# A fused decoder layer on one core: first transposition of the probabilities behind the first scores, and VectorE's first key remainders behind the reciprocals

## The reference, cut to what matters

```python
sim = jnp.einsum('bhid,bhjd->bhij', q, k) * SCALE
attn = jax.nn.softmax(sim, axis=-1)
out = jnp.einsum('bhij,bhjd->bhid', attn, v)
x = _layernorm(x + out_projected)
```

## Time and profile before

| | us |
|---|---|
| median of 3 runs | 1244.94 (1244.93 to 1247.97) |
| the profiled execution, its own time | 1244.77 |
| its span (first to last instruction) | 1242.9 |
| TensorE busy | 1201.6 (97%) |
| VectorE busy | 863.6 (69%) |
| ScalarE busy | 555.1 (45%) |
| GpSimd busy | 584.7 (47%) |

### The profile page before, as it was taken

The page is one execution under the profiler, slowest core; times in us unless marked ns, Lnnn a source line. Parts: engine busy times, 40 slices in busy tenths (PEclk is TensorE's granted clock), DMA queues, the critical chain, the costliest instruction groups (busy, mean ns, idle before and its releaser), DMA issues.

```text
span 1242.9 us, 27255 instructions
## 1 busy us (share of the span) xinstructions
PE 1201.6 (97%) x10512; PEld 1050.0 (84%) x10512; DVE 863.6 (69%) x1694; ACT 555.1 (45%) x1097; POOL 584.7 (47%) x968
## 2 busy tenths in 40 slices
PE   8986999999999999999999999989999999999998
PEld 7865888888888888888888888877799899899888
DVE  5555988989889889889888898988523423432435
ACT  2123556555555555565565555545523412421420
POOL 2233665666666566656666576655322112202201
PEclk9997999999999999999999999999999999999999
DMA  9821012011111111120110111310222011021001
GB/s 274 225 63 35 20 51 61 19 60 44 35 52 53 34 54 44 35 60 20 60 50 30 59 46 35 125 39 26 95 69 69 1 69 69 1 69 69 1 1 35
DMA packets 88740, 70.07 MB, mean 56 GB/s; under 512 B 41379, under 2 KB 82084, under 8 KB 88613
## 3 DMA queue, kind: packets, MB, share of 16 engines
q1 hardware_dynamic: 86580, 67.67, 17.9%
q10 hardware_dynamic: 2032, 0.66, 0.2%
HBM read 42.09 MB, written 26.22 MB: 55 GB/s over the span
## 4 chain that ended last, share of the span: by engine, by line
PE 70%; POOL 8%; issue 8%; DVE 6%; ACT 1%; POOLq 0%; DVEq 0%
PE sim L137 6%; PE sim L138 6%; PE sim L139 6%; PE ob L137 5%; PE ob L139 5%; PE ob L138 5%; PE pt L499 4%; PE pw L393 3%; PE pt L139 2%; PE pt L138 2%; PE pt L137 2%; PE pw L456 2%; PE pw L137 2%; POOL prob L965 2%; PE pw L139 2%
## 5 line engine op out<-in xcount | busy, mean ns | idle before, releaser
L1616 POOL TENSOR_TENSOR w_lo<-w_raw,w_hi 128x2048 fp32r<-128x2048 f32 x16 | 73.7, 4610 | 221.0 <-ACT w_hi L1556 167.8
L137 PE MATMUL ob<-b_hi,pT_hi 128*128 128x256 f32 x512 | 151.5, 296 | 0.0
L138 PE MATMUL ob<-b_lo,pT_hi 128*128 128x256 f32 x512 | 144.1, 281 | 0.0
L139 PE MATMUL ob<-b_hi,pT_lo 128*128 128x256 f32 x512 | 144.1, 281 | 0.0
L965 POOL TENSOR_TENSOR prob<-prob,rz 128x512 f32<-128x512 f32 x128 | 130.9, 1043 | 12.4 <-DVE rz L816 12.4
L732 ACT ACTIVATE pT_hi<-pt 128x512 fp32r<-128x512 f32 x128 | 76.1, 595 | 112.0 <-PE pt L499 111.3
L726 ACT ACTIVATE prob<-prob 128x512 f32<-128x512 f32 x128 | 81.1, 633 | 95.5 <-DVE prob L870 95.4
L137 PEld LDWEIGHTS ob<-b_hi,pT_hi 128*128 128x128 f32 x512 | 97.4, 190 | 8.3 <-issue 5.4
L138 PEld LDWEIGHTS ob<-b_lo,pT_hi 128*128 128x128 f32 x512 | 97.6, 191 | 1.8
L139 PEld LDWEIGHTS ob<-b_hi,pT_lo 128*128 128x128 f32 x512 | 96.9, 189 | 0.0
L635 ACT ACTIVATE x<-h,nmr,rstd 128x256 f32<-128x256 f32 x128 | 76.5, 598 | 41.6 <-POOL nmr L891 24.4
(11 more groups left out here) (244 smaller groups left out, 3720.4 us busy)
## 6 DMA issues: line engine op xcount, KB each, us to landing
xraw<-in_x SPq DMA_DIRECT2D x16, 512.0 KB, 4.0
kv_scratch<-stage SPq DMA_DIRECT2D x32, 256.0 KB, 3.5
x_scratch<-x SPq DMA_DIRECT2D x64, 128.0 KB, 1.7
out_x<-o_sb SPq DMA_DIRECT2D x64, 128.0 KB, 1.7
w_raw<-in_L_ffn_experts_inter SPq DMA_DIRECT2D x8, 1024.0 KB, 5.1
w_raw<-in_L_ffn_experts_out SPq DMA_DIRECT2D x8, 1024.0 KB, 7.8
kraw<-kv_scratch SPq DMA_DIRECT2D x16, 256.0 KB, 2.9
vraw<-kv_scratch SPq DMA_DIRECT2D x16, 256.0 KB, 2.8
```

Of the source, the lines that this page charges most:

```text
L137: pe.matmul(out, lh, rh, start=first, stop=False)
L138: pe.matmul(out, lh, rl, start=False, stop=False)
L139: return pe.matmul(out, ll, rh, start=False, stop=last)
```

## The change

Four places are edited. On TensorE the first transposition of tile n-1 (`pe_pT` half 0) goes behind the first scores of tile n (`pe_sim` half 0). On ScalarE `act_pT` half 0 goes behind `act_norm` of layernorm 1. On VectorE `dve_pT` half 0 goes behind the first maximum, the preparation place 2 and the first shift. And VectorE's `A0` and `A2` go from place 5 to a new place 6, behind the reciprocals.

```diff
-        "A0": ((2, 2), (2, 3), (2, 5)), "A2": ((2, 2), (2, 3), (2, 5)),
+        "A0": ((2, 2), (2, 3), (2, 6)), "A2": ((2, 2), (2, 3), (2, 6)),
...
+        if has_sim:
+            pe_sim(pe, it, slot, 0)
         if has_prev:
             pe_pT(pe, n - 1, (slot - 1) % 2, 0)
-        if has_sim:
-            pe_sim(pe, it, slot, 0)
         prep(1)
...
         prep(0)
-        if has_prev:
-            act_pT(act, n - 1, 0)
         if has_x1T:
...
             act_norm(act, 1, 1 - q, h1[:, 1 - q, :], x1[:, par(1 if slot else 0), (slot - 1) % 4, 1:C + 1], "x1_ready")
+        if has_prev:
+            act_pT(act, n - 1, 0)
         prep(1)
...
         prep(1)
-        if has_prev:
-            dve_pT(dve, n - 1, 0)
         if has_sim:
             dve_max(dve, n, 0)
         prep(2)
         if has_sim:
             dve_shift(dve, n, q, 0)
+        if has_prev:
+            dve_pT(dve, n - 1, 0)
         prep(3)
...
             dve.reciprocal(rz[:, q, :], zsum[:, :]).then_inc(s["rz_made"], 1)
+        prep(6)
         if has_z:
             need(dve, "z_made", n + 5)
```

## The result

The changed kernel takes 1311.68 us (median of 4 runs, 1310.05 to 1312.03), the kernel before 1245.58 (4 runs, 1244.93 to 1247.97). The ratio is 1.0527, with a 95% interval of 1.051 to 1.0543: 66 us slower. The profiled execution took 1312.03 us, its span is 1310.3 us, and its mean granted clock is 0.981 (before 0.992).

A forecast was written before the change was run, and what follows sets the result against it. TensorE was taken to set a batch's time, 48.6 us, so its new waits are paid in full. The parts sum as 28 + 23.5 + 2.5 - 1 = 53 us on 1244.77, giving 1298, range 1276 to 1316.

The forecast's parts named there:

- forecast's own 1284 to 1306: Whole kernel: range of the forecast by itself, each part about half-way to its bounds, chance 0.68.
- Part 1: Slot 0: half 1 waits 2.0 us more as Q1 stands in its chain, 14 times, 28 us.
- Part 2: Slot 2: folded keys A1 and A3 wait 1.57 us for VectorE's A0 and A2, 15 iterations, 23.5 us.
- Part 3: Slot 3: wait for probabilities goes, but half 0's remainder comes 0.17 us later, 14 times, 2.5 us.
- removed wait for `prob`: Start of slot 3: TensorE's 0.28 us wait for GpSimd's probabilities goes, with 1.4 us of scores ahead.
- Part 4: Slot 1: B2 and B3 push half 1 back, so cost 0, with 0.7 us of cover.
- Part 5: Last two batches: scores fill waits for probabilities, but half 1 waits for pT_lo; -1 us, bounds -4.5 and +3.
- rival 2: Slots 0 and 2: only one of the two new waits comes, 1270 to 1275 us; chance 0.12.
- rival 1: TensorE's clock falls at the new waits: 1322 us at all 14 long ones, 1305 to 1315 at some; chance 0.12.

The follow-up runs named there:

- e1: Changed kernel with VectorE's A0 and A2 back at place 5, in front of pT_lo: 1279.46 us, ratio 1.0279.
- e4: Changed kernel with Q1's ScalarE copy ahead of x and its VectorE remainder behind pT_lo: 1277.91 us, ratio 1.0266.
- e2: Kernel before with only VectorE's A0 and A2 moved to place 6, behind the reciprocal: 1269.13 us, ratio 1.0201.
- e6: Kernel before with TensorE's first scores ahead of the transposition in slot 3 only: 1245.69 us, ratio 1.0008.
- e9: Kernel before with e6's TensorE order, and SB and SW earlier on ScalarE, SB's remainder earlier on VectorE: 1245.53 us, ratio 1.0001.
- e3: Changed kernel with the six matmuls of slot 0's second scores done twice, from the second batch on: 1296.1 us, ratio to before 1.0419.
- e5: Kernel before with the transposition behind the first scores on TensorE only, ScalarE and VectorE in old order: 1268.0 us, ratio 1.0184.
- e10: Kernel before with SB and SW earlier on ScalarE and SB's remainder earlier on VectorE, TensorE's order untouched: 1245.42 us, ratio 0.9998.

## Why the prediction came out as it did

**The forecast of slower held; 1298 was 14 us short of 1311.7.** The time lies in the range that was given, but above the forecast's own 1284 to 1306, and the step that failed is the one that put the clock at nothing.

**Part 1 (28 us), right.** Every link came as worked out, half 1 5.33 instead of 5.25 us after the slot's start. Only `x`, taken as ready there, is not: ScalarE waits for GpSimd's `nmr` (375.53, idle 1.43), but it has 0.51 us to spare before `pT_hi`, so the chain doesn't see it. e1 (the order alone, 2.23 a batch with slot 3's part) and e4 (without `Q1`, 1.6 a batch back) show it from both sides.

**Part 2 (23.5), right.** `A1` waits 1.45 us idle. e2 gives 1.51 a batch, net of the wait that went and the one that came; 1.57 was forecast.

**Part 3 (2.5), right in the sum, wrong in the reading.** A1 to half 1 takes 0.25 us more than before, 0.17 forecast. But the prediction speaks of the removed wait for `prob` as a gain that a later remainder takes back. e2, e6 and e9 take it away in other orders and get nothing for it either. The likely reason is that the stretch from `A1` to `Q0` hangs on VectorE, but that is not shown.

**Part 4 (0), right.** No wait in slot 1 stands in the list.

**Part 5 (-1), too small a gain.** From the last L393 group to the end it is +3.6. This part still holds one long wait of slot 0 and two for the keys, 2.0 + 2 x 1.57 = 5.1, and one fall of the clock, 1.6: 6.7. So 3 us came back, within the bound of -4.5. The waits for `prob` (6.5 us in five before) are 0.5 in one, and the clock fell once here instead of twice. Most of that gain was taken back by the transposition's waits for `pT_lo`, as the part feared. Before, from 745 us on:

```profile
PE pt L499 <- DVE pT_lo L877: 1.5, 1, 1.5
```

and in the changed kernel, from 809 us on:

```profile
PE pt L499 <- DVE pT_lo L878: 9.0, 8, 1.9
```

**A batch** takes 52.3 to 52.4 us where the clock stays full: the forecast's 52.4.

**The bounds.** The forecast's own 1284 to 1306 does not come out of the parts' bounds: half-way to each gives 1280 to 1307. And the range of 1276 to 1316 takes in nothing of rival 2, which ends at 1275. Neither touches the sum.

**The clock (0 in the sum; rival 1, chance 0.12).** It fell in 9 of the 14 iterations with the long wait. Each fall cost 54.0 - 52.35, some 1.65 us; rival 1 had 1.7. Nine times that is 15 us, and e3 measures 15.6; the two profiled executions differ by 16.2, nine falls and the one at the start. Without the nine the kernel would have taken some 1297, against the sum of 1298. The right place was between forecast and rival 1, in that rival's "1305 to 1315", and its chance should have been much higher: my argument against it was that 2.0 is shorter than 2.28, and no row said that 2.0 is short enough. The Trainium skill's "TensorE: Matmul & The Clock Gate", section "A second HAM failure mode: psum-queue depth-cycling", describes a clock that goes up and down with idle times repeated in each iteration; the trace agrees, with 0.53 after the wait and 1.00 later in the same batch (384 to 434 us).

**The missing 1.5 us at the start** has the same cause, and shows how little of it the wait alone decides. This is TensorE's L393 group at 76 us in the changed kernel,

```profile
76.16 4.54 PE L393 MATMUL pw<-xraw 128*128 128x257 f32 x16 [2.07 <-POOL x L1097]
```

and this the same one in the kernel before:

```profile
76.12 2.87 PE L393 MATMUL pw<-xraw 128*128 128x257 f32 x16 [2.07 <-POOL x L1096]
```

The same wait of 2.07 us, the same work, and once half the speed. Of the twelve traces, four have this fall (the changed kernel, e4, e5 and e10), though up to there all of them wait alike, 1.98 to 2.07 us. Going by that, these 1.5 us are not a cost of the change.

**Still open** is what decides it. Waits of 1.95 us were followed by a lowered clock in 9 of 14 batches of the changed kernel and in 4 of 14 of e1. I take all waits of TensorE of 1.2 us and more that the twelve traces have from 120 to 960 us, and the one at 76 us. None of the 79 that are shorter than 1.9 us went with a lowered clock, 17 of the 44 between 1.9 and 2.1 us did, and 12 of the 22 between 2.2 and 3.0. One of 3.00 us did not (e6, at 833.68). So the length alone does not decide. In e1 the falls stand at every fourth of the 14 equal waits (215.03, 419.80, 624.56 and 829.30 us). Its last two, first without and then with the fall; the four matmuls of the transposition take 0.63 and then 0.90 us:

```profile
778.50 0.63 PE L499 MATMUL pt<-ident,prob 128*128 128x128 f32 x4 [1.95 <-DVE pT_lo L878]
829.30 0.90 PE L499 MATMUL pt<-ident,prob 128*128 128x128 f32 x4 [1.94 <-DVE pT_lo L878]
```

Spacing so even under equal waits suggests that the moment at which a wait comes counts too. No run here shifts that moment alone.

## What to carry to other kernels

A transposition that moves behind other work takes its copy and its remainder with it, and whatever stands between their two new places in the ScalarE and VectorE lists comes into the chain that frees the bank; write out that chain link by link; here it came out to a tenth of a microsecond. A short wait of the busiest engine is not a gain until one has seen what comes next: here a wait of 0.3 us came back as another in three different orders. And where a wait of some 2 us on TensorE can't be avoided, price it twice, once for itself and once for the clock that may fall behind it (1.6 us each time here), or fill it with matmuls that do no harm.

## What the hardware did that I had not expected

A kernel that does 90 matmuls more (10602 instead of 10512, six in each of 15 batches) is 15.6 us faster than the one that waits in their place (1296.1 and 1311.68 us). And the same wait before the same instructions is followed by a lowered clock in one kernel's trace and not in the other's (4.54 and 2.87 us for the same 16 matmuls after 2.07 us of waiting).
